# Attention output of two head pairs at a time: one full PSUM bank every fourth step in place of half a bank every second

## The reference

```
xn  = layernorm(x)                                   # both branches start from it
q   = (layernorm(xn)*g + b) @ Wq ; k, v = xn @ Wkv   # 16 heads of 64
k,v = [2 null keys/values ; k,v]
sim = 8 * l2norm(q)*q_scale . l2norm(k)*k_scale - slope_h*|i-j|, causal
att = softmax(sim) @ v @ Wout
ffn = silu(xn@sg.T)*(xn@su.T)@sd.T + top-2 of 8 experts (sigmoid router, weights normalised)
out = x + att + ffn
```

## Time and profile before

| | |
|---|---|
| timed runs, us | median 478.66 (478.4 to 479.74, 3 runs) |
| the profiled execution | 479.73 us, its span on the core 478.0 us |
| busy, share of the span | PE 421.6 us (88%), PEld 64%, DVE 366.7 (77%), ACT 357.9 (75%), POOL 294.3 (62%) |
| mean granted TensorE clock | 0.961 |

### The profile page before, as it was taken

One profiled execution on the slowest core, in us unless ns is written; L12 is line 12 of the kernel. 1 busy time (PEld: TensorE's weight loads), 2 busy tenths in 40 slices (PEclk: granted clock), 3 DMA queues, 4 the chain that ended last, 5 costly groups with the idle time before them and its releaser, 6 DMA issues.

```text
span 478.0 us, 10590 instructions
## 1 busy us (share of the span) xinstructions
PE 421.6 (88%) x2793; PEld 305.1 (64%) x2793; DVE 366.7 (77%) x1419; ACT 357.9 (75%) x1097; POOL 294.3 (62%) x444
## 2 busy tenths in 40 slices
PE   3846805999998899999999999999999999999995
PEld 3734503667776676676666776776676677767663
DVE  5699602666652898899799889989988997997884
ACT  3344702666665979988997998899799899989874
POOL 3748779910001589579768848966875894785400
PEclk9969855999999999999999999999999999999998
DMA  8971112222221000000001001000100100010000
GB/s 234 319 247 34 56 49 60 62 73 81 77 73 39 1 25 0 2 24 23 3 1 45 2 1 47 0 2 2 44 2 2 45 2 2 14 32 2 24 23 12
DMA packets 29738, 21.36 MB, mean 45 GB/s; under 512 B 3528, under 2 KB 27376, under 8 KB 29552
## 3 DMA queue, kind: packets, MB, share of 16 engines
q1 hardware_dynamic: 26816, 16.46, 11.7%
q0 software_dynamic: 2048, 4.20, 2.9%
q10 hardware_dynamic: 816, 0.03, 0.1%
HBM read 12.41 MB, written 8.26 MB: 43 GB/s over the span
## 4 chain that ended last, share of the span: by engine, by line
PE 54%; DVE 18%; issue 9%; ACT 8%; POOL 7%; DMA 3%; ACTq 1%; DVEq 0%
POOL slot_x L418 7%; PE bank L1104 7%; PE bank L1095 7%; PE bank L958 6%; PE bank L959 5%; PE bank L960 5%; DVE arena_b L887 4%; PE bank L1053 4%; PE bank L1085 4%; PE bank L1172 4%; PE bank L1118 4%; DVE arena_b L902 3%; DMA arena_b<-slot_x 2%; DVE probT L912 2%; DVE ssq L871 2%
## 5 line engine op out<-in xcount | busy, mean ns | idle before, releaser
L663 ACT ACTIVATE arena_b<-arena_b,nmx 128x130 f32<-128x130 f32 (+1 forms) x256 | 114.9, 458 | 16.3 <-PE bank L1095 8.3
L887 DVE CUSTOM_DVE_ANT_0 arena_b<-bank,bias 128x130 f32<-128x130 f32 (+1 forms) x256 | 81.2, 355 | 29.8 <-PE bank L1104 15.7
L902 DVE TENSOR_SCALAR arena_b<-arena_b,rden 128x130 f32<-128x130 f32 (+1 forms) x256 | 84.9, 375 | 4.5
L431 POOL TENSOR_TENSOR rpow<-ssm,mhalf 128x8 f32<-128x8 f32 x32 | 52.5, 1641 | 45.3 <-DVE ssm L875 45.3
L444 POOL TENSOR_TENSOR arena_b<-arena_b,rnorm 128x512 f32<-128x512 f32 x64 | 66.9, 1045 | 5.1 <-POOL rnorm L434 0.2
L1095 PE MATMUL bank<-ident,arena_b 128*128 128x128 f32 x384 | 67.0, 283 | 2.4 <-DVE arena_b L902 2.3
L1104 PE MATMUL bank<-arena_a 64*128 64x130 f32 (+1 forms) x512 | 59.5, 351 | 0.8 <-ACT arena_a L624 0.8
L1095 PEld LDWEIGHTS bank<-ident,arena_b 128*128 128x128 f32 x384 | 44.1, 141 | 22.0 <-DVE arena_b L902 13.1
L428 POOL TENSOR_TENSOR rnorm<-ssm,mhalf 128x8 f32<-128x8 f32 x32 | 52.7, 1646 | 0.9
L663 ACT ACTIVATION_READ_ACCUMULATOR arena_b<-arena_b,nmx 128x1 f32 x256 | 51.2, 200 | 0.0
L871 DVE TENSOR_REDUCE ssq<-arena_b 128x8 f32<-128x512 f32 x64 | 43.6, 682 | 4.7 <-ACT arena_b L601 3.9
(11 more groups left out here) (196 smaller groups left out, 969.4 us busy)
## 6 DMA issues: line engine op xcount, KB each, us to landing
slot_x<-probT SPq DMA_DIRECT2D x3, 832.0 KB, 8.6
arena_b<-slot_x SPq DMA_DIRECT2D x39, 64.0 KB, 1.9
slot_y<-arena_b SPq DMA_DIRECT2D x39, 64.0 KB, 1.5
arena_a<-in_L_attn_x_dram SPq DMA_DIRECT2D x2, 512.0 KB, 5.3
arena_b<-in_L_ffn_wd_dram SPq DMA_DIRECT2D x1, 1024.0 KB, 9.9
arena_b<-in_L_attn_Wkv_dram SPq DMA_DIRECT2D x1, 1024.0 KB, 8.8
arena_b<-in_L_attn_x_dram SPq DMA_DIRECT2D x8, 128.0 KB, 2.6
out_dram<-arena_b SPq DMA_DIRECT2D x8, 128.0 KB, 2.0
```

The costliest lines, as they stand in the source:

```text
L663: sc.activation(prob[:, (HEADS * b + h) % RP, c], sim[h % 2][:, c], ACT.Exp, scale=-1.0, bias=nmx[:, h % HEADS, t:t + 1], accum_out=den[:, ...
L887: ve.tensor_tensor_reduce(out=sim[h % 2][:, c], in0=bank[h % 2][:, c], in1=bias[:, c], scale=-SLOPES[h], scalar=3e38, op0=ALU.add, op1=ALU ...
L902: ve.tensor_scalar(pr, pr, rden[:, h % HEADS, t:t + 1], None, ALU.mult).then_inc(g.pn, 1)
```

## The change

Two pairs now share one output: `ofour` is all of bank 4, the first pair in columns 0 to 255 and the second in 256 to 511. At lag 4 of every fourth head (h % 4 == 3, so at steps 7, 11, 15 and at step 3 of the next batch) TensorE issues the output products of both pairs, one behind the other. One step later ScalarE copies all 512 columns to `oT[f % 2]`, which is twice as wide, and two steps later TensorE issues both projection products. `probT` has two buffers for each of even and odd heads, so that the first pair's probabilities stay until the second's are there, and their copies wait for the group of four before. `pvd`, `oev` and `oread` count groups of four. The table of side jobs, VectorE's order and GpSimd's order are unchanged.

```
-        probT = [sb(f"probT{i}", [P, 3 * P]) for i in range(2)]
+        probT = [[sb(f"probT{half}_{i}", [P, 3 * P]) for i in range(2)] for half in range(2)]
...
-        oT = [sb(f"oT{i}", [P, SEQ]) for i in range(2)]
-        opair = bank[4][:, 0:SEQ]
+        oT = [sb(f"oT{i}", [P, 2 * SEQ]) for i in range(2)]
+        ofour = bank[4]
...
# ScalarE
-                    if h is not None and h % 2:
-                        p = h // 2
-                        act.wait_ge(g.pvd, PAIRS * b + p + 1)
-                        if part != "first" or p >= 2:
-                            act.wait_ge(g.oread, PAIRS * b + p - 1)
-                        sc.activation(oT[p % 2][:], opair, ACT.Copy).then_inc(g.oev, 1)
+                    if h is not None and h % 4 == 3:
+                        f = h // 4
+                        act.wait_ge(g.pvd, FOURS * b + f + 1)
+                        if part != "first" or f >= 2:
+                            act.wait_ge(g.oread, FOURS * b + f - 1)
+                        sc.activation(oT[f % 2][:], ofour[:], ACT.Copy).then_inc(g.oev, 1)
...
# TensorE, lag 4
-                    if h is not None and h % 2:
-                        p = h // 2
-                        if part != "first" or p >= 1:
-                            pe.wait_ge(g.oev, PAIRS * b + p)
-                        for half, evacuated in ((0, g.ptev_d), (1, g.ptev_a)):
-                            pe.wait_ge(evacuated, PAIRS * b + p + 1)
-                            r, hh = slice(half * DH, (half + 1) * DH), 2 * (p % PAIRS) + half
-                            te.matmul(opair[r, 0:SEQ], v[:, 0, hh * DH:(hh + 1) * DH], probT[half][:, 0:SEQ], start=True, stop=False)
-                            ins = te.matmul(opair[r, P:SEQ], v[:, 1, hh * DH:(hh + 1) * DH], probT[half][:, SEQ:3 * P],
-                                            start=False, stop=True)
+                    if h is not None and h % 4 == 3:
+                        f = h // 4
+                        if part != "first" or f >= 1:
+                            pe.wait_ge(g.oev, FOURS * b + f)
+                        for p in (2 * f, 2 * f + 1):
+                            o = p % 2 * SEQ
+                            for half, evacuated in ((0, g.ptev_d), (1, g.ptev_a)):
+                                pe.wait_ge(evacuated, PAIRS * b + p + 1)
+                                r, hh, pT = slice(half * DH, (half + 1) * DH), 2 * (p % PAIRS) + half, probT[half][p % 2]
+                                te.matmul(ofour[r, o:o + SEQ], v[:, 0, hh * DH:(hh + 1) * DH], pT[:, 0:SEQ], start=True, stop=False)
+                                ins = te.matmul(ofour[r, o + P:o + SEQ], v[:, 1, hh * DH:(hh + 1) * DH], pT[:, SEQ:3 * P],
+                                                start=False, stop=True)
                         ins.then_inc(g.pvd, 1)
...
# TensorE, lag 6
-                        pe.wait_ge(g.oev, PAIRS * b + p + 1)
-                        te.matmul(bank[6][:, 0:SEQ], wo[:, p % PAIRS, :], oT[p % 2][:], start=p == 0,
-                                  stop=p == -1).then_inc(g.oread, 1)
+                        pe.wait_ge(g.oev, FOURS * b + f + 1)
+                        for p in (2 * f, 2 * f + 1):
+                            ins = te.matmul(bank[6][:, 0:SEQ], wo[:, p % PAIRS, :], oT[f % 2][:, p % 2 * SEQ:(p % 2 + 1) * SEQ],
+                                            start=p == 0, stop=p == -1)
+                        ins.then_inc(g.oread, 1)
```

More of the change, by code:

```diff
@@ L23 @@
 PAIRS = HEADS // 2
+FOURS = HEADS // 4
 K0 = NNULL + P
@@ L187, in build @@
         nk2, nv2 = sb("nk2", [32, 2, DH]), sb("nv2", [32, 2, DH])
-        nvT = probT[1][:, 0:PAIRS * 36]
-        zeros = probT[0][:, 0:DIM]
+        nvT = probT[1][0][:, 0:PAIRS * 36]
+        zeros = probT[0][0][:, 0:DIM]
         S = {n: sem(n) for n in [
@@ L620, in side_out @@
                     if c == 0 and part != "ready":
-                        act.wait_ge(g.pvd, PAIRS * b + PAIRS // 2)
+                        act.wait_ge(g.pvd, FOURS * b + FOURS // 2)
                     if c == 1 and part != "first":
-                        act.wait_ge(g.pvd, PAIRS * b)
+                        act.wait_ge(g.pvd, FOURS * b)
                     sc.activation(v[:, t, c * 512:(c + 1) * 512], side[i][:], ACT.Copy).then_inc(left[i], 1)
@@ L648, in entry @@
                         act.wait_ge(g.ptps, HEADS * b + h + 1)
-                        if part != "first" or h >= 2:
-                            act.wait_ge(g.pvd, PAIRS * b + h // 2)
-                        sc.activation(probT[1][:], bank[3][:, 0:3 * P], ACT.Copy).then_inc(g.ptev_a, 1)
+                        if part != "first" or h >= 4:
+                            act.wait_ge(g.pvd, FOURS * b + h // 4)
+                        sc.activation(probT[1][h // 2 % 2][:], bank[3][:, 0:3 * P], ACT.Copy).then_inc(g.ptev_a, 1)
                     if s == 6 and "prev" in whose:
-                        act.wait_ge(g.oread, PAIRS * b)
+                        act.wait_ge(g.oread, FOURS * b)
                         act.wait_ge(g.fin, b)
@@ L909, in entry @@
                         dve.wait_ge(g.ptps, HEADS * b + h + 1)
-                        if part != "first" or h >= 2:
-                            dve.wait_ge(g.pvd, PAIRS * b + h // 2)
-                        ve.tensor_copy(probT[0][:], bank[2][:, 0:3 * P]).then_inc(g.ptev_d, 1)
+                        if part != "first" or h >= 4:
+                            dve.wait_ge(g.pvd, FOURS * b + h // 4)
+                        ve.tensor_copy(probT[0][h // 2 % 2][:], bank[2][:, 0:3 * P]).then_inc(g.ptev_d, 1)
                     if s % 2 == 0:
@@ L1112, in entry @@
                     h = head_at(part, s, 6)
-                    if h is not None and h % 2:
-                        p = h // 2
-                        if p == 0 and part != "first":
+                    if h is not None and h % 4 == 3:
+                        f = h // 4
+                        if f == 0 and part != "first":
                             pe.wait_ge(g.yev, b)
-                        pe.wait_ge(g.oev, PAIRS * b + p + 1)
-                        te.matmul(bank[6][:, 0:SEQ], wo[:, p % PAIRS, :], oT[p % 2][:], start=p == 0,
-                                  stop=p == -1).then_inc(g.oread, 1)
+                        pe.wait_ge(g.oev, FOURS * b + f + 1)
[3 more added lines that the diff above has]
+                        ins.then_inc(g.oread, 1)
                     if s == 13 and "own" in whose:
```

## The result

The changed kernel takes 483.8 us (482.77 to 484.99, 6 runs) where the kernel before takes 478.54 (478.03 to 480.24, 6 runs): a ratio of 1.0104 [1.0084, 1.0123], so 1.0% longer, clear of the noise. The forecast had 480.5, 474.5 to 483.5: the direction was right, the size was not. The profiled execution took 483.42, its span is 481.7, the mean granted clock 0.962 as before (0.961).

A forecast was written before the change was run, and what follows sets the result against it. The prediction took the bound to change within each batch: GpSimd's chain, then ScalarE's side copies, then TensorE. It added 1.3 us (seven batches at +0.18) and 0.56 at the end to 478.66, giving 480.5 us, range 474.5 to 483.5.

The forecast's parts named there:

- The side copies of step 12: Steps 11 to 13: ScalarE's longer output copy delays its second side copy, so step 13's projection starts 0.15 us later.
- the freed 1.37 us of TensorE: Steps 11 to 13: output projection (0.43) and output group (0.96) gone from TensorE, but the time was filling a wait.
- the 18 waits of the earlier trace: Waits on ScalarE's second side copy, read as showing that TensorE's wait for it at step 13 is real.
- TensorE from step 13 to the scores of step 4: Stretch into the next batch, taken as TensorE bound: moved work and a vanished 0.31 us stall sum to +0.03 us.
- Take this stretch as fixed from the scores of step 4: Steps 4 to 11: GpSimd's chain sets the time and hides TensorE's saving of 0.19 us, so no change.
- the sign that the prediction had named: GpSimd's first norm of step 4 moving against that step's scores would mean steps 4 to 11 are not fixed.
- Seven such stretches: The +0.18 us per batch counted seven times, for batches 0 to 6: +1.3 us.
- Earlier steps of the last batch … I take 0: Last batch before its end: TensorE's gain of some tenths taken back by ScalarE and VectorE; bounds 0 and -0.5, taken as 0.
- the end at 0.56: Program end: longer last copy (+0.13) and one more last product (+0.43), together +0.56 us.
- Rival 1: Tiling-mode drains on TensorE are the bound: 1.24 us saved per batch, 470.5 us, or 475 with half; chance 0.25.
- Rival 2: Lost and saved time cancel in each batch within 0.1 us, leaving the end alone: 478.7 to 479.5 us; chance 0.17.

The follow-up runs named there:

- second_group: Kernel before with only pairs 2 and 3 grouped: outputs at step 11, one 512-column copy at step 12, two products at step 13; last batch as before; 483.54 us.
- last_by_pair: Changed kernel with its last batch as before the change, outputs, copies and projections pair by pair; 482.04 us, 1.0069 of the kernel before.
- last_two: Kernel before with only pairs 6 and 7 grouped: outputs at step 3, one copy at step 4, two products at step 5; last batch as before; 476.16 us.
- first_group: Kernel before with only pairs 0 and 1 grouped: outputs at step 7, one copy at step 8, two products at step 9; last batch as before; 478.91 us.
- last_two_4_later: last_two with the product of pair 4 also moved from step 15 to step 1; 475.0 us, 0.9906 of the kernel before.

## Why the prediction was wrong

- **The side copies of step 12: right.** The projection of step 13 came 0.16 later, forecast 0.15, behind the copy that was named, and most of the freed 1.37 us of TensorE became idle time (0.24 and 0.98 in the rows above). second_group has the 0.16 without the other groups. One sign was misread: of the 18 waits of the earlier trace rows none is TensorE's at step 13 of batches 1 to 6. Nine lie ahead of the batches, three in batch 0, and six are weight loads at step 12, 0.33 us each, ahead of which TensorE's products had no idle time.
- **TensorE from step 13 to the scores of step 4: right piece by piece, within a tenth.** In A: 0.16, then 0.43 at step 13, then 0.69-0.43=0.26 at step 15 (forecast 0.22): 0.85, measured 0.86, forecast 0.80. In B: step 1 gives back 0.53, as forecast; steps 3 and 4 give 0.10 (forecast 0.31-0.22=0.09).
- **"Take this stretch as fixed from the scores of step 4": wrong by 0.11.** The second norm starts 4.02 after the scores (286.44-282.42) instead of 3.91, the sign that the prediction had named. At step 4 ScalarE's 512-column copy stands ahead of the exponentials; that it is the cause is not shown. What is fixed, within the limits above, is C, from the second norm on: 24.93 to 24.98 in 12 of the other 19 kernels. With these tenths a batch costs 0.86-0.53=0.33 (0.34 by the batches) instead of 0.18.
- **"Seven such stretches" and "Earlier steps of the last batch … I take 0", with the end at 0.56: these steps failed.** A's loss is paid at seven ends of a batch, B's gain is had in six. From step 0 to step 14 of the last batch the scores fell back by another 0.10 where the others gain half a microsecond: with the output group gone from step 1, and no projection for a next batch behind it, TensorE waits for ScalarE, as in the row below. The end then cost 1.27, the doubled products ahead of the last transposes included, which I had not counted. By the parts: 7x0.86-6x0.53+0.10+1.27=4.2, forecast 7x0.18+0.56=1.8. Of the 2.4 missed, 0.5 are the seventh gain that was not had, 0.8 the last batch, and 1.1 the tenths of the points above, seven times. In the trace of last_by_pair, with the products of the last batch single again, the end from step 14 on is back to that of before within 0.01; the 0.10 ahead of it became 0.53.

Timeline of PE in the last batch, step 1:

```profile
440.47 0.66 PE L1054 MATMUL bank<-ident,arena_b 128*128 128x128 f32 x4 [0.36 <-ACT arena_a L615]
```

The two traces differ by 3.7 us, of which -0.6 lies ahead of the batches: 4.3 from there on, of the 5.0 that the ratio gives. The other 0.7 is within what executions of one kernel differ by (spans of after 481.0 to 483.2) and is not explained further.

Rival 1, the drains as the bound: of the 0.31 us per group 0.27 is saved (a second pair costs 0.69, a single group 0.96). In last_two TensorE makes 0.70 less in B, these 0.27 and a product of 0.43 moved to step 5, and B is 0.52 shorter; saved beside the chain (first_group) it is worth nothing. Rival 2 named the right kind of sum, terms that nearly cancel; they did not.

Open: what exactly sets B's floor of 12.48 (ScalarE runs without a break from step 2 on in before, and all six kernels at the floor have its 512-column copy at step 4, but no run relieved it there), and the 0.2 of C in last_two_4_later.

## What to carry to other kernels

Find the chain that does not move, here GpSimd's from its second to its eighth norm, and price only what lies between its end and its next start; work beside it can be moved in or out for nothing only in part: 0.86 us at step 9 cost the middle batches nothing, 1.29 at step 5 lengthened the chain itself by 0.54. Grouping saves a fixed price per group but it also moves work: of four groups one gained 0.5 us per batch, one nothing, and two lost 0.6 each, so try them one at a time and keep the one. Count the batches at both ends by themselves: a loss at the end of a batch and a gain at the start of the next do not occur equally often.

## Not expected of the hardware

- VectorE's short operations that met GpSimd's 1.04 us multiplication lasted to its end (0.17 became 1.05), while the two-piece normalisation that ran beside GpSimd's 1.64 us norm took its usual 0.55: in after at 290.30, with the norm from 289.78 to 291.42. So a shift of some tenths can add or remove up to 0.9 us at one place. That the multiplication holds them is the reading given above.
- TensorE starts the passes of two column halves, listed one half after the other in the program, interleaved (four L1088 ahead of the first L1089), also where two pairs are queued (1.50 us for both).
